# A fused Mamba-2 block and product-key expert layer on one core: expert rows scaled on ScalarE and summed on TensorE by transposes

## The reference

```
x = layernorm(x + mamba2(x))        # z, xBC, dt = u @ W_in; conv of 4 taps, silu; scan over
                                    # 16 heads; gate by silu(z); rms norm; y @ W_out
h = silu(x @ W_up.T + b_up) @ W_down.T + b_down          # 512 -> 2048 -> 256
q = h @ W_q.T                       # 2 x 8 heads x 64
scores, idx = top_k(q . keys, 8)    # each half of each head against 64 keys
sc, pk = top_k(all 64 pair sums, 8) # 8 of 4096 experts in each of 8 heads
z = silu((h . down_embed[indices]) * softmax(sc))        # 64 coefficients a token
x = layernorm(x + sum over the 64 picks of z * up_embed[indices])
```

## Time and profile before

| what | value |
|---|---|
| device time, median of 3 runs | 3161.11 us |
| lowest, highest | 3151.85, 3166.98 us |
| the profiled execution | 3151.04 us, its span 3149.2 us |
| busy share of the span: PE, DVE | 89%, 88% |
| busy share of the span: ACT, POOL | 65%, 65% |
| mean granted clock of PE | 0.953 of full |
| DMA engines | 272 GB/s, about 0.8 busy |

### The profile page before, as it was taken

How to read it: one execution, slowest core, us unless ns; L and a number is a source line. 1 busy time by engine, 2 the same in 40 slices (tenths; PEclk the granted TensorE clock), 3 DMA queues, 4 the chain that set the end, 5 groups by cost and what they waited for, 6 DMA issues and landing times.

```text
span 3149.2 us, 44785 instructions
## 1 busy us (share of the span) xinstructions
PE 2790.8 (89%) x11776; PEld 1737.3 (55%) x11776; DVE 2777.5 (88%) x10160; ACT 2049.7 (65%) x6513; POOL 2062.7 (65%) x2056
## 2 busy tenths in 40 slices
PE   7989899998898999999899989899898999898863
PEld 4565456655555655555566545556555565555541
DVE  3489899998899999999899989999999999899986
ACT  3466766666776666676666676666676666677642
POOL 0066666676676667666667666666766666766676
PEclk9999999999999999999999999999999999999986
DMA  8088888888888888888888888888888888888888
GB/s 284 23 263 275 270 279 273 277 290 282 272 285 265 270 292 287 276 282 277 265 277 297 273 276 271 273 278 290 284 277 268 276 272 288 283 278 281 277 303 272
DMA packets 189855, 856.76 MB, mean 272 GB/s; under 512 B 36192, under 2 KB 39392, under 8 KB 189088
## 3 DMA queue, kind: packets, MB, share of 16 engines
q0 software_dynamic: 163840, 805.44, 77.0%
q1 hardware_dynamic: 19104, 34.87, 3.2%
q10 hardware_dynamic: 6656, 13.60, 1.2%
HBM read 845.38 MB, written 8.39 MB: 271 GB/s over the span
## 4 chain that ended last, share of the span: by engine, by line
PE 38%; DVE 32%; DMA 9%; POOL 9%; issue 7%; ACT 5%; POOLq 0%; SPq 0%; DVEq 0%; ACTq 0%
DVE bank L1143 14%; POOL ring L276 9%; DMA ring<-embed,idx 9%; PE bank L500 8%; DVE ring L1129 8%; PE bank L359 7%; DVE xc L974 6%; PE bank L339 5%; PE bank L441 4%; PE bank L488 4%; PE bank L368 3%; ACT xc L679 1%; PE bank L376 1%; PE bank L307 1%; ACT xskip L691 1%
## 5 line engine op out<-in xcount | busy, mean ns | idle before, releaser
L276 POOL DMA_INDIRECT ring<-embed,idx x2048 | 2061.4, 1007 | 1074.8 <-issue 532.3
L1143 DVE SCALAR_TENSOR_TENSOR bank<-ring,coef,bank 128x512 f32<-128x512 f32 x1312 | 992.4, 756 | 7.4 <-issue 0.2
L1129 DVE SCALAR_TENSOR_TENSOR ring<-ring,hcur 128x256 f32<-128x256 f32 x2048 | 823.8, 423 | 138.5 <-DMA ring<-embed,idx 136.1
L645 ACT ACTIVATE coef<-prob,zp 128x1 f32<-128x1 f32 x2048 | 456.0, 286 | 630.8 <-DVE ring L1129 625.4
L500 PE MATMUL bank<-ring,diag_c 128*128 128x512 f32 x1344 | 672.8, 631 | 115.9 <-ACT diag_c L654 101.3
L463 PE MATMUL bank<-zs,w_up 128*128 128x128 f32 x4096 | 502.2, 287 | 69.2 <-ACT zs L767 65.8
L463 PEld LDWEIGHTS bank<-zs,w_up 128*128 128x128 f32 x4096 | 496.2, 203 | 110.2 <-ACT zs L767 91.8
L500 PEld LDWEIGHTS bank<-ring,diag_c 128*128 128x128 f32 x1344 | 247.2, 199 | 379.2 <-issue 223.7
L974 DVE SCALAR_TENSOR_TENSOR xc<-raw,taps,xc 128x128 f32<-128x128 f32 x960 | 266.2, 351 | 102.6 <-ACT xc L679 102.5
L339 PE MATMUL bank<-w_in,ut 128*128 128x512 f32 (+1 forms) x768 | 285.8, 524 | 4.0 <-ACT seg L667 3.9
L654 ACT ACTIVATE diag_c<-cst,coef 128x128 f32<-128x128 f32 x672 | 234.8, 394 | 48.4 <-PE bank L500 38.0
(11 more groups left out here) (144 smaller groups left out, 3422.2 us busy)
## 6 DMA issues: line engine op xcount, KB each, us to landing
ring<-embed,idx POOLq DMA_INDIRECT x2048, 4.6
ring<-uT SPq DMA_DIRECT2D x4, 2048.0 KB, 14.2
ut<-uT SPq DMA_DIRECT2D x32, 256.0 KB, 6.5
zs<-u SPq DMA_DIRECT2D x32, 256.0 KB, 5.6
out<-acc SPq DMA_DIRECT2D x32, 256.0 KB, 4.6
w_up<-W_upT ACTq DMA_DIRECT2D x1, 4096.0 KB, 13.0
w_in<-W_in ACTq DMA_DIRECT2D x1, 2560.0 KB, 17.4
w_in<-W_in ACTq DMA_DIRECT2D x1, 2048.0 KB, 22.0
```

The costliest lines, as they stand in the source:

```text
L276: pool.indirect_dma_start(out=ring[:, k % RING, :], out_offset=None, in_=embed, in_offset=bass.IndirectOffsetOnAxis(ap=idx[:, half, k:k + ...
L645: m = act.activation(coef[:, k:k + 1], prob_v[:, k:k + 1], ACT.Silu, scale=zp[:, k:k + 1])
L1129: m = dve.scalar_tensor_tensor(out=ring[:, k % RING, 0:DP], in0=ring[:, k % RING, 0:DP], scalar=1.0, in1=hcur[:, :], op0=ALU.mult, op1=ALU ...
L1143: dve.scalar_tensor_tensor(out=total if n == len(DVE_ROWS) - 1 else running[:, :], in0=ring[:, k % RING, DP:ROW], scalar=coef[:, k:k + 1], ...
```

## The change

1. ACT no longer makes a diagonal matrix for a P row. It writes the row's 512 numbers, times the coefficient, into one of four buffers `scaled`, which are not part of the ring. The slot of the ring is free as soon as this is done (`scaled_ok`), no longer when PE is done.
2. PE adds the scaled row to bank 5 by four 128 x 128 transposes (accumulating), so bank 5 holds the transposed sum. A transpose is one instruction of the trace. Once a tile ACT copies bank 5 to SBUF (`copy_sum`), PE transposes it back into bank 0 (`turn_back`), and `back_sum` reads bank 0. `turn_back` stands behind the second half of `out_proj`.
3. 25 rows of a tile are P rows instead of 21: one each in groups 7, 9, 11 and 12 moves from DVE to PE.
4. On PE, group 13 now stands between the halves of `z_proj`, and group 14 behind `step_sums` instead of behind `turn_x`.
5. On ACT, the coefficients of group 2 come before the square root of the gated norm.
6. The SBUF space kept for the descriptors of POOL's transfers is 8192 bytes a partition, passed as an argument; before, none was passed and the default stood. `diag_c` (4 x 128 numbers) goes, `rows_t` of the same size and `scaled` (4 x 512) come.

```diff
+SCALED = 4
+DMA_SCRATCH = 8192
-DIAGS = 4
-GROUPS = ("DD", "PPPD", "DD", "DDD", "PPD", "DDD", "DD", "DDD", "PDDD", "DDD", "DDD", "DDDD", "PDD", "PPPD", "PP", "PDD", "PPPP", "D", "DDD", "PPPD", "D", "PDD")
+GROUPS = ("DD", "PPPD", "DD", "DDD", "PPD", "DDD", "DD", "PDD", "PDDD", "PDD", "DDD", "PDDD", "PPD", "PPPD", "PP", "PDD", "PPPP", "D", "DDD", "PPPD", "D", "PDD")
...
                         if j in PE_ROWS:
-                            pool.wait_ge(row_pe, NPG * of + signal_of(j))
+                            pool.wait_ge(scaled_ok, len(PE_ROWS) * of + PE_ROWS.index(j) + 1)
...
                 for k in rows_of(g, "P"):
                     n = PE_ROWS.index(k)
-                    pe.wait_ge(diag_ok, len(PE_ROWS) * t + n + 1)
+                    pe.wait_ge(scaled_ok, len(PE_ROWS) * t + n + 1)
                     if n == 0 and not first:
-                        pe.wait_ge(sum_ok, 3 * t - 2)
-                    m = pe.matmul(bank[SUM][:, :], diag_c[:, (len(PE_ROWS) * t + n) % DIAGS, :], ring[:, k % RING, DP:ROW],
-                                  start=(n == 0), stop=(n == len(PE_ROWS) - 1))
+                        pe.wait_ge(sum_t, t)
+                    for c in range(KD):
+                        m = pe.matmul(bank[SUM][:, c * P:(c + 1) * P], scaled[:, (len(PE_ROWS) * t + n) % SCALED, c * P:(c + 1) * P], ident,
+                                      start=(n == 0 and c == 0), stop=(n == len(PE_ROWS) - 1 and c == KD - 1),
+                                      is_transpose=True, skip_group_check=True)
...
+            def turn_back(t):
+
+                pe.wait_ge(sum_t, t + 1)
+                pe.wait_ge(yT_ok, 2 * min(t + 3, NT))
+                if t > 0:
+                    pe.wait_ge(sum_ok, 3 * t - 2)
+                for c in range(KD):
+                    m = pe.transpose(bank[BACK][:, c * P:(c + 1) * P], rows_t[:, c, :], ident)
+                m.then_inc(back_mm, 1)
...
                 if ahead:
                     out_proj(i + 1, False, 1)
+                if not first:
+                    turn_back(i - 1)
                 new(1, 2, 3)
...
-                    if len(PE_ROWS) * t + n >= DIAGS:
-                        act.wait_ge(row_pe, NPG * (t - (n < DIAGS)) + signal_of(PE_ROWS[n - DIAGS]))
-                    act.activation(diag_c[:, (len(PE_ROWS) * t + n) % DIAGS, :], ident, ACT.Copy, scale=coef[:, k:k + 1]).then_inc(diag_ok, 1)
+                    if len(PE_ROWS) * t + n >= SCALED:
+                        act.wait_ge(row_pe, NPG * (t - (n < SCALED)) + signal_of(PE_ROWS[n - SCALED]))
+                    act.activation(scaled[:, (len(PE_ROWS) * t + n) % SCALED, :], ring[:, k % RING, DP:ROW], ACT.Copy,
+                                   scale=coef[:, k:k + 1]).then_inc(scaled_ok, 1)
+
+            def copy_sum(t):
+
+                act.wait_ge(row_pe, NPG * (t + 1))
+                if t > 0:
+                    act.wait_ge(back_mm, t)
+                act.activation(rows_t[:, :, :], bank[SUM][:, :].rearrange("p (a c) -> p a c", a=KD), ACT.Copy).then_inc(sum_t, 1)
...
             def back_sum(t):
                 dve.wait_ge(row_used, len(DVE_ROWS) * (t + 1))
-                dve.wait_ge(row_pe, NPG * (t + 1))
-                dve.tensor_tensor(total, total, bank[SUM][:, :], ALU.add).then_inc(sum_ok, 1)
+                dve.wait_ge(back_mm, t + 1)
+                dve.tensor_tensor(total, total, bank[BACK][:, :], ALU.add).then_inc(sum_ok, 1)
...
-    nc = bacc.Bacc("TRN2", target_bir_lowering=False, num_devices=1)
+    nc = bacc.Bacc("TRN2", target_bir_lowering=False, num_devices=1, dynamic_dma_scratch_size=DMA_SCRATCH)
```

More of the change, by code:

```diff
@@ L108, in build @@
         ring = sb("ring", [P, RING, ROW])
+        scaled = sb("scaled", [P, SCALED, D])
         ut = sb("ut", [P, D])
@@ L139, in build @@
         coef = sb("coef", [P, PICKS])
-        diag_c = sb("diag_c", [P, DIAGS, P])
+        rows_t = sb("rows_t", [P, KD, P])
         st6b = sb("st6b", [P, 6])
@@ L163, in build @@
         Y_BANKS, ST_BANKS, YT_BANKS, OP, XBC_BANKS = (6, 7), (4, 1), (2, 0), 6, (7, 2, 0)
-        X1T, UP_BANKS, DOWN, HT, SIM_BANKS, SUM = 6, (4, 1, 7, 2), 6, 6, (7, 6), 5
+        X1T, UP_BANKS, DOWN, HT, SIM_BANKS, SUM, BACK = 6, (4, 1, 7, 2), 6, 6, (7, 6), 5, 0
         running = bank[3]
@@ L201, in build @@
         xr_mm, xr_ok, skip_ok = sem("xr_mm"), sem("xr_ok"), sem("skip_ok")
-        yT_ok, sq_ok, rms_ok, ln_ok, x1T_ok, h1_ok, hT_ok, exp_ok, hcur_ok, coef_ok, diag_ok, ln2_ok, saved_ok = (
+        yT_ok, sq_ok, rms_ok, ln_ok, x1T_ok, h1_ok, hT_ok, exp_ok, hcur_ok, coef_ok, scaled_ok, ln2_ok, saved_ok = (
             sem(n) for n in ("yT_ok", "sq_ok", "rms_ok", "ln_ok", "x1T_ok", "h1_ok", "hT_ok", "exp_ok", "hcur_ok",
-                             "coef_ok", "diag_ok", "ln2_ok", "saved_ok"))
+                             "coef_ok", "scaled_ok", "ln2_ok", "saved_ok"))
+        sum_t, back_mm = sem("sum_t"), sem("back_mm")
         cur_ok, conv_ok, cbm_ok, xdt_ok, g_ok, xdec_ok, yoff_ok, y_half, y_ok, dcy_ok, st_ok, rr_ok, bn_ok, x1_ok, h_ok = (
@@ L350, in turn_xbc @@
                         pe.wait_ge(yT_ok, 2 * i)
+                    if XBC_BANKS[part] == BACK and i >= 3:
+                        pe.wait_ge(sum_ok, 3 * i - 8)
                 for c in range(4 * part, min(4 * part + 4, KC)):
@@ L541, in tile @@
                     z_proj(i + 1, 0)
-                    z_proj(i + 1, 1)
                 old(13)
                 if ahead:
+                    z_proj(i + 1, 1)
                     step_sums(i + 1, 0)
@@ L548, in tile @@
                     step_sums(i + 1, 3)
+                old(14)
+                if ahead:
                     turn_x(i + 1)
-                old(14, 15)
+                old(15)
                 if ahead:
@@ L599, in _ @@
                 weighted(NT - 1, g, False)
+            turn_back(NT - 1)
         @block.scalar
@@ L865, in tile @@
                     turn_y(i + 1)
+                if not first:
+                    copy_sum(i - 1)
                 new(0, 1)
@@ L868, in tile @@
                     gated_squares(i + 1)
+                new(2)
+                if ahead:
                     gated_rms(i + 1)
-                new(2)
                 if not first:
@@ L904, in _ @@
                 coefs(NT - 1, g)
+            copy_sum(NT - 1)
             back_sqrt(NT - 1)
```

2 lines of the change are left out of this document (1 added, 1 removed).

## The result

The changed kernel takes 3210.17 us (median of 4 runs, 3209.63 to 3211.79), the kernel before, timed beside it, 3159.94 (4 runs, 3151.85 to 3166.98): a ratio of 1.0161, 95% interval 1.0136 to 1.0186. It is slower by 50 us. The forecast was 3215.

What follows compares the result with a forecast made beforehand. Bound: a loop handing on between engines, PE and DVE nearly full. +1.9 us a pass over 30 passes (+57), last tile -3: 3205 us profiled, 3215 on the median's scale; forecast case 3180 to 3265, wider range 3120 to 3285.

Steps and rivals of the forecast that it cites:

- (a): ACT, group 4: `coefs` 2.3 us late and two scalings (+0.6) delay `xbc_copy`; x, B, C projection's third part +2.6 us.
- (b): The chain over ACT's taps to x1's copy has no P row and stays: up projection +2.6 us.
- (c): To the down projection's end PE has three rows of 0.45 instead of one of 0.86, +0.5; PE sets h, +3.1.
- (d): Groups 11 and 12 (+0.5), then three rows between `z_proj`'s halves: second half and second gate come 4.9 us later.
- (e): ACT from second gate to `state_decay`: 11 P rows raise 23.8 us to 27.2, idle 0.8 left; 28.0 us in all.
- (f): End of pass: copy 0.58, then `out_proj` starts at 1673.3 instead of 1671.13, +2.2 us; taken as +1.9 a pass.
- The ring: POOL's wait for PE (289.2 us) goes nearly wholly; costed at nothing in the loop, without cover up to 4.4 us a pass.
- The faster rival: DVE sets the pace: four rows give 2.8 us a pass, earlier refills up to 4.4 more; 3077 us, chance 0.21.
- The transposes and the clock: On PE, skill page: 104 transposes replacing 42 matmuls bring more half rate; the sum instead took only gaps to matter.
- Much slower by the clock: Half rate behind PE's gaps in two places more: +3 us a pass beside the +1.9, 3305 us, chance 0.13.
- No change: ACT's idle time goes entirely, scaling costs half (1.7 us less): loss under 0.5 us a pass, 3150 to 3177, chance 0.16.
- The descriptor space: Half the space holds up POOL; gathers taking half as much again would give 3850 us, chance 0.02.

Runs made afterwards that it cites:

- both mends: Changed kernel with `xbc_copy(0)` ahead of group 4's coefficients and `turn_back` between the halves of `out_proj`: 3027.19 us, 0.9592 of the kernel before.
- the kernel before with the copy first: Kernel before with only ACT's `xbc_copy(0)` moved ahead of group 4's coefficients: 3143.27 us, 0.9969 of the kernel before.
- Five experiments: Changed kernel with `turn_back` early (4064.18, again 4091.78 us), `xbc_copy(0)` early (3924.05), both (4022.87); kernel before with 8192-byte descriptor space (3666.92).
- The three programs: Changed kernel with `xbc_copy(0)` ahead of group 4's coefficients (3924.05 us), `turn_back` between `out_proj`'s halves (4064.18), or both edits (4022.87).

## Why the prediction was right, point by point

- *PE relieved by 6.4 us a pass.* PE's busy time fell from 2790.8 to 2674.7 us, 3.7 a pass (of 31). With both mends, where no half-rate spell sits in the projection, it is 2579.5, 6.8 a pass. The term was right; in the changed kernel 49 us went into the projection at half rate (285.8 to 335.2 us).
- *DVE -2.8, ACT +6.9.* Measured over 31 passes: (2777.5 - 2697.8) gives 2.6, (2265.3 - 2049.7) gives 7.0. A scaling takes 715 ns, 0.32 over the diagonal; I took 0.31.
- *The new wait of 1.3 to 2.3 us at `back_sum`.* 63.3 us in 30 times, 2.1 each, as forecast.
- *(a) third part +2.6.* 19.94 instead of 17.3 us in the pass shown, +2.6; in the medians of 26 passes 20.0 and 17.5, +2.5. Not in the sum: it then ran at half rate, so that the projection ended 4.4 and not 2.6 us later. That is the step that was mis-sized, by the mechanism which I had named under the clock (gaps hurt) and not put into the walk.
- *(b), (c).* So the up projection was 4.8 instead of 2.6 us later. It gave a part back, since it now ran at full clock: at the down projection's end the delay is 3.9 (I had 3.1), at h 3.5, and PE sets h as I had it.
- *(d) second gate +4.9.* 5.3.
- *(e) 28.6 us from the gate's start to `state_decay`'s end.* 28.5 (before 30.6): 2.1 us of the delay are caught there, and 3.2 are left at `state_decay`'s end (I had 2.7).
- *(f) +1.9 a pass.* +2.1 in the mean, +59 in the span (3208.3 - 3149.2); 57 - 3 was forecast.
- *The ring, costed at nothing.* Right for this kernel: 71 us less waiting of DVE for rows, and none of it reached the end. Both mends show that a gain lay hidden behind the stand and ACT's order. They take off 183 us: the 50 that were lost, and some 130 more. Not all of that is the change's own, since the copy's place gives 12 us without it. The fair measure is the kernel before with the copy first, 3143 us, beside 3027: 116 us, 3.7 a pass, of which 26 are the up projection's busy time (509.9 and 483.6). The faster rival had 2.8 us a pass, with up to 4.4 more. How the 116 us divide between DVE's four rows, PE and the ring wasn't tried.
- *The transposes and the clock.* By the Trainium skill (TensorE: Matmul & The Clock Gate, Part 4: PE-mode transpose) transposes do not count as PE being busy in the way that matmuls do. Here are the windows of the changed kernel behind a gap, with 16 transposes of rows as nearly all the work of the second window, and PE's timeline there:

```profile
1682.50:1686.00 3.50, 0.00 (x0) 0.00 (x0) 3.40 (x5) 3.44 (x9) 0.28 (x1) 1.00 0.75 270
1686.00:1689.60 3.60, 3.56 (x17) 3.54 (x18) 3.00 (x15) 3.60 (x12) 2.74 (x3) 0.53 0.41 111
1689.60:1693.50 3.90, 3.90 (x40) 3.90 (x40) 3.49 (x10) 3.87 (x14) 2.95 (x4) 1.00 0.88 280
```

```profile
1686.04 3.55 PE L506 MATMUL bank<-cst,scaled 128*128 128x128 f32 x16 [3.87 <-ACT scaled L676]
1689.39 0.39 PE L417 MATMUL bank<-cst,xskip 128*128 128x128 f32 x1
```

  The clock was 0.53 of full over the 3.6 us behind the gap, with hardly anything but transposes on PE, and 1.00 from 1689.60 on, 0.2 us after the first matmul began. So the transposes did not keep it at 1.2 GHz, and the trace does not bear that sentence out here. With both mends the mean is 0.941 beside 0.953 before, with 3,328 transposes more. By the rows the half rate stands behind gaps, as the sum had it; that not every gap brings it, the two up projections above show.
- *What would show it.* The stand (30 times, not 31), the price of a scaling, the wait of the third part (3.3 us a pass, a little over the 2 to 3 named) and passes of 95 us came. ACT is at 71%, not near 75%. POOL's wait for PE went, but its waits for ACT (169.1 us) and DVE (313.6, before 88.2) are not small: a gather that is free of one reader waits for the next. And the clock fell to 0.913, which I had named as a sign against the forecast. The time was right all the same, and partly by luck, because errors offset each other: the projection ended 1.8 us later than I had, the up and down projections gave 0.9 back where I had 0.5 more, and from the down projection's end to the second gate 1.4 us were lost instead of 1.8.
- *The rivals.* Much slower by the clock: the mechanism was there, at one place and not two, and its price there 1.6 us a pass (49.4 us in 31), about half of the 3 that I gave to two places. No change and faster: not in this kernel. The descriptor space: 3850 us is excluded; a part of up to 1% is not.

## What to carry to other kernels

When work is moved off an engine, look first at the last operation of the new path: four transposes, 0.6 us, placed at the far side of 8 us of matmuls, with a copy that stood behind coefficients and scalings, turned a gain of 4% (12 us of it from the copy's place alone) into a loss of 1.6%. Put such a hand-back in front of the block that the receiver doesn't need, and put copies that a matmul block waits for ahead of work that depends on late data. And when a term of relief is costed at nothing because a new wait covers it, note it as what removing the wait may bring back: here some 116 us beyond the loss itself. Two edits whose times add up need not cure two things; a table of where each pass stands tells them apart.

## What of the hardware was not expected

- Five experiments, on two chips, had every kernel 15% slower or more: in some stretches PE's matmuls began only every 0.7 or 1.4 us, as in the three rows of the timeline above. The kernel before lost 480 us (3640 beside 3160). The three programs with 1,984 more matrix instructions and as many more weight loads lost 820 to 1000 (3924, 4064 and 4023 beside 3105, 3129 and 3027 for the same programs later), and their ratios were 1.07 to 1.13 instead of 0.96 to 0.99. They have 17% more matrix instructions than the kernel before and lost 1.7 to 2.1 times as much, so the loss does not go by the number of these instructions alone; its cause stays open. Only the kernel before, timed beside them, gave it away.
- Transposes of a float32 tile 128 x 128 that accumulate in PSUM follow each other in 0.11 to 0.12 us (12 in 1.47 us at full clock); a group of 16 behind a gap, at half rate, took 3.55 us, 0.22 each.
